# Block-sparse attention on eight cores: the projection of the next head pair moved into the last chunk of the current one, and the block-maximum pass started earlier with doubled buffers

## The chip, the cores and the metric

The kernel runs on the 8 cores of one Trainium2 chip. Every core runs the same program on its own 2 of the 16 sequences, and no core talks to another. The metric is device time in microseconds of the slowest core.

## The reference, cut to what matters

One layer: a layer norm, then attention plus a feed-forward block, both added to the input. The attention is exact on the best-scoring 32x32 blocks and coarse elsewhere.

```
xn = layernorm(x)                       # 16 x 2048 x 1024, 16 heads of 64
Q, K, V = heads(xn @ W.T + b)           # per head: 2048 x 64, 64 blocks of 32 rows
low  = mean(Qb) @ mean(Kb).T * SCALE    # 64 x 64 block scores
hi_mask = the 1024 best blocks (with the diagonal band)
blk_rmax = max of hi scores per row; max_vals = max over the row's chosen blocks
attn = exp(hi - max_vals);  low_attn = exp(low - row_max - 10000*hi_mask) * 32
out  = (hi_out*hi_corr + low_out*low_corr) / (hi_norm*hi_corr + low_norm*low_corr + 1e-6)
x + out + sigmoid(xr @ Wr.T) * (relu(xk @ Wk.T)**2 @ Wv.T)
```

## The kernel before, in words

The program writes the instruction list of each engine by hand, in Python order. `Rec.emit` appends an instruction and, on every engine but TensorE, first makes it wait for the engine's own previous instruction; `Rec.wait` makes an engine wait until another engine's counter has reached a value. There is one counter per engine (sPE, sDV, sAC, sSY for the sync queue's transfers, sGP for GpSimd's transfers, sGC for GpSimd's arithmetic). So each queue runs in program order, and the transfers that GpSimd issues go one at a time: the next is issued when the last has landed.

The first 2255 us (layer norm, weight transposes, block selection by bisection, feed-forward) are not touched by the change. After that a loop over 8 head pairs `p` runs. A pair has four units of attention `bhs[0]` to `bhs[3]` (two heads times two sequences), and goes through these stages:

- **QK projection** (lines 979 to 995): 16 groups of 8 matmuls of 512 columns make `qtp` and `ktp` from the normalised input `xnT`; ScalarE evacuates each group. The groups use the two halves (slots) of the PSUM tile `pA` in turn.
- **V projection and transposes** (from line 1006): twice 4 groups of 8 matmuls of 512 columns into `pA`, evacuated to `vTf` (line 1025), and after each four groups 16 transposing matmuls (line 1045) into `pS` with two ScalarE copies each (lines 1054 and 1058). Between the transposes stands phase A of `bhs[0]`, two units per transpose.
- **Phase A** of one `bhs` (`emit_phaseA_half`, 64 units): a matmul of 512 columns of Q·K into one half of `pA` (line 748), a VectorE maximum over blocks into `bm` (line 756), and after every fourth unit the mask `bx` is added (line 763) and the maximum taken (line 766). After unit 63, VectorE and ScalarE make `eps_all` (lines 771 to 777). `bx` and `rmb` are loaded per `bhs` by `emit_prep_bx` on GpSimd (lines 692 and 696); there is one buffer of each, so the load waits for the end of phase A of the `bhs` before (`phA_done_dv`), and the first unit of a phase A waits for its `bx`.
- **Four chunks** `i` = 0 to 3, one per `bhs`, of 32 iterations `kg` (`emit_chunk_iter`): two score matmuls into `pS` (line 823), the two output matmuls of the iteration before (line 791, `emit_av`, which wait for its exponential), up to two units of phase A of a later `bhs`, and the exponential of 128x1024 on ScalarE (line 838). Halfway and at the end ScalarE evacuates `pO` to `outT` (line 810). `emit_prep` loads the `rhsc` and `lhsc` operands of the next chunk on GpSimd (lines 705 and 707). The epilogue of a chunk transposes and scales; half of it is put off to `kg` 4 of the next chunk. At the end of a pair, GpSimd adds two tiles (lines 950 and 953), the result is stored, and sync, TensorE and VectorE wait for everything.

Units of phase A before, by stage: `bhs[0]` all 64 in the V stage; chunk 0: 64 of `bhs[1]`; chunk 1 from `kg` 8: 48 of `bhs[2]`; chunk 2 from `kg` 8: 16 of `bhs[2]`, then 32 of `bhs[3]`; chunk 3 in `kg` 8 to 23: 32 of `bhs[3]`. In chunk 3 the iterations 24 to 31 have none.

Of the kernel before, what the change touches and what calls it, by code (L numbers as in the profile page):

```python
# [9 lines left out]
F32 = mybir.dt.float32  # L10
# [85 lines left out]
def build_program(debug=False, trunc=None):  # L96
# [36 lines left out]
    with stack:  # L133
# [503 lines left out]
        with contextlib.ExitStack() as st_p2:  # L637
# [15 lines left out]
            bm = sb("bm", [128, 64], F32)  # L653
            bmm = sb("bmm", [128, 64], F32)
            bx = sb("bx", [128, 1024], F32)
            rmb = sb("rmb", [128, 16], F32)
# [15 lines left out]
            def bh_idx(p, hip, s):  # L672
# [9 lines left out]
                     "nac_la": [0, 0], "ngp_prep": [0, 0], "ndv_prep": [0, 0], "ngp_bx": 0,  # L682
                     "nac_la_last": 0, "ngp_prep_last": 0,
                     "prev_exp": [0, 0], "phA_dv": 0, "phA_done_dv": 0,
                     "nst_a": 0, "ngp_rmb": 0, "prev_exp2": [0, 0], "phA_dv2": [0, 0], "nac_ep": 0,
# [3 lines left out]
            def emit_prep_bx(p, hip, sq):  # L689
                b = bh_idx(p, hip, sq)  # L690
                r.wait("gpsimd", "sDV", state["phA_done_dv"])
                state["ngp_bx"] = r.emit("gpsimd", lambda e, b=b: e.dma_start(
                    bx[:, :],
                    bsm_dram[b].rearrange("j t k -> j (t k)")
                    .unsqueeze(1).broadcast_to([4, 32, 1024])))
                state["ngp_rmb"] = r.emit("gpsimd", lambda e, b=b: e.dma_start(
                    rmb[:, :],
                    rm_dram[b].unsqueeze(1).broadcast_to([4, 32, 16])))

            def emit_prep(p, hip, sq, par, prev_chunk_pe, with_bx=False):  # L700
# [7 lines left out]
                    lhs2[par][0:64, :], ktp[p0:p0 + 64, ts0:ts0 + S]))  # L708
                if with_bx:
                    emit_prep_bx(p, hip, sq)  # L710
# [20 lines left out]
                state["ngp_prep"][par] = state["ngp_rmb"]  # L731
                state["ndv_prep"][par] = ngp5

            def emit_phaseA_half(p, hip, sq, u):
                b = bh_idx(p, hip, sq)
                p0 = 64 * hip
# [19 lines left out]
                nred = r.emit("vector", lambda e, kq=kq, half=half: e.tensor_reduce(  # L756
                    bm[:, kq * 16:(kq + 1) * 16],
                    pA[:, half * 512:(half + 1) * 512]
                    .rearrange("p (k e) -> p k e", e=32),
                    axis=AX.X, op=ALU.max))  # L760
                state["phA_dv2"][half] = nred
                if kq == 3:
                    r.emit("vector", lambda e, b=b, t=t: e.tensor_tensor(  # L763
                        bmm[:, :], bm[:, :], bx[:, t * 64:(t + 1) * 64], ALU.add))
# [4 lines left out]
                if u == 63:  # L769
                    r.wait("vector", "sGP", state["ngp_rmb"])  # L770
# [3 lines left out]
                    ndv_e = r.emit("vector", lambda e: e.tensor_tensor(  # L774
                        epst[:, :], epst[:, :], rmb[:, :], ALU.max))
                    r.wait("scalar", "sDV", ndv_e)
                    r.emit("scalar", lambda e, b=b: e.activation(
                        eps_all[:, b * 16:(b + 1) * 16], epst[:, :],
                        AF.Exp, bias=clneps[:, :]))
                    state["phA_done_dv"] = ndv_e  # L780
# [180 lines left out]

            state["nls_next"] = 0
            for p in range(8):
# [7 lines left out]
                r.wait("scalar", "sPE", r.cnt["sPE"])  # L971
                r.wait("scalar", "sGP", r.cnt["sGP"])
                r.wait("tensor", "sSY", nls)
                pcons = state["pcons"]
                for tag, dst in [("q", qtp), ("k", ktp)]:
                    for n in range(8):
                        slot = n % 2
                        r.wait("tensor", "sAC",
                               max(pcons[slot], state["pA_free_ac"][slot]))
                        r.wait("tensor", "sDV",  # L980
# [83 lines left out]
                for i in range(4):  # L1064
# [4 lines left out]
                    for kg in range(32):  # L1069
# [3 lines left out]
                        elif i == 1:  # L1073
                            if kg == 0:
                                emit_prep_bx(*bhs[2])
# [100 lines left out]
```

How the kernel before makes its waits and increments, by code:

```python
    def emit(self, eng, fn):  # L57
        sname = ESEM[eng]
        n = 16 if eng in ("sync", "gpsimd") else 1
        if eng != "tensor" and self.cnt[sname]:
            self.wait(eng, sname, self.cnt[sname])
        self.cnt[sname] += n
        h = self.sem[sname]
        self._push(eng, lambda e, fn=fn, h=h, n=n: fn(e).then_inc(h, n))
        return self.cnt[sname]
# [1 line left out]
    def wait(self, eng, sname, val):  # L67
        if not val:
            return
        h = self.sem[sname]
        self._push(eng, lambda e, h=h, v=val: e.wait_ge(h, v))
```

## Time and profile before

| what | value |
|---|---|
| median of 2 runs | 6025.58 us (6016.91 to 6034.24) |
| the profiled execution | 6024.37 us; span of its slowest core 6022.5 us |
| spans of the 8 cores | 5990.2 to 6022.5 us |
| mean granted TensorE clock, by core | 0.751 to 0.756 of full |
| busy: PE, DVE, ACT | 52%, 41%, 28% of the span |

All views below are of core 1, the slowest. Times are microseconds from the start of its span. PE is TensorE's matmul stream, PEld its weight loads, DVE is VectorE, ACT ScalarE, POOL GpSimd, SPq the sync queue. PEclk is the granted share of TensorE's full clock of 2.4 GHz; 0.50 is 1.2 GHz. An engine that is idle is only a loss where the next thing that ends last stands behind it.

### The profile page before, as it was taken

Reading aid. Unit: us, or ns where it says so; the run is one execution under the profiler, and the core shown is the slowest. Engines: PE = TensorE matmul, PEld = TensorE weight load, DVE = VectorE, ACT = ScalarE, POOL = GpSimd, SP = SyncE. Lnnn points to the kernel's source line nnn. Section 1 sums busy time; section 2 is a strip of 40 time slices with the busy share of each in tenths; the row PEclk is TensorE's granted clock in tenths of the full one; section 3 lists DMA queues with packets and bytes.
Section 4 is the critical chain, followed back from the end, with each engine's and each line's share of the span. In section 5 each row is a group of like instructions: output and inputs, shape, how many; then the busy total and the mean of one; then the engine's idle time right before and its main releaser. Section 6 shows DMA issues by size and latency. Waiting matters only on the chain.

```text
span 6022.5 us, 57635 instructions; the slowest of 8 cores (5990.2 to 6022.5 us)
## 1 busy us (share of the span) xinstructions
PE 3157.4 (52%) x11513; PEld 1112.4 (18%) x11513; DVE 2488.4 (41%) x5263; ACT 1708.7 (28%) x2627; POOL 281.9 (5%) x301
## 2 busy tenths in 40 slices
PE   1121113333333426765766676676676667666676
PEld 0021101111111102221222222122122122122121
DVE  3421224433444224543643543543552642543454
ACT  2200000000000002542442443443344344254254
POOL 0000010000000000000000000000000000000000
PEclk9965556777676856886886887777787787687687
DMA  1233001121111211011010110100110010010010
GB/s 62 67 74 80 2 16 42 42 49 44 40 42 40 61 41 25 20 22 28 17 25 22 24 25 20 25 22 15 25 25 20 18 32 17 21 31 18 17 27 18
DMA packets 516779, 190.09 MB, mean 32 GB/s; under 512 B 494282, under 2 KB 495474, under 8 KB 516274
## 3 DMA queue, kind: packets, MB, share of 16 engines
q1 hardware_dynamic: 482386, 130.46, 9.5%
q0 software_dynamic: 34080, 55.95, 4.2%
q8 instruction: 136, 2.23, 0.2%
q14 instruction: 177, 1.45, 0.1%
HBM read 142.23 MB, written 39.34 MB: 30 GB/s over the span
## 4 chain that ended last, share of the span: by engine, by line
PE 37%; DMA 19%; DVE 17%; ACT 14%; issue 11%; DVEq 1%; POOL 1%; ACTq 1%; SPq 0%; POOLq 0%
PE pA L748 9%; PE pS L823 9%; ACT aT L838 7%; PE pO L791 7%; DVE bm L756 5%; PE pA L984 4%; PE pA L516 4%; DMA bx<-bsm_dram 3%; DMA fW<-wT_r 3%; ACT stage L916 2%; DMA nb<-norm_all 2%; DVE fA L501 2%; DMA fW<-wT_v 2%; DMA fW<-wT_k 2%; PE pA L1017 1%
## 5 line engine op out<-in xcount | busy, mean ns | idle before, releaser
L756 DVE TENSOR_REDUCE bm<-pA 128x16 f32<-128x512 f32 x2048 | 1416.7, 692 | 1321.4 <-PE pA L748 1164.2
L838 ACT ACTIVATE aT<-pS 128x1024 bf16<-128x1024 f32 x1024 | 1048.7, 1024 | 974.1 <-PE pS L823 938.3
L748 PE MATMUL pA<-ktp,qtp 64*128 64x512 bf16 x2048 | 883.3, 441 | 632.2 <-DMA bx<-bsm_dram 252.0
L791 PE MATMUL pO<-aT,vtm 128*65 128x512 bf16 x2048 | 714.7, 435 | 360.5 <-ACT aT L838 358.5
L823 PE MATMUL pS<-rhsc,lhsc 128*128 128x512 bf16 x2048 | 725.4, 443 | 29.0 <-DVE rhsc L712 29.0
L516 PE MATMUL pA<-fA,fW 128*128 128x512 bf16 x1536 | 412.7, 421 | 276.8 <-DMA fW<-wT_r 65.0
L748 PEld LDWEIGHTS pA<-ktp,qtp 64*128 64x128 bf16 x2048 | 190.1, 95 | 1334.3 <-issue 1330.9
L417 PE MATMUL pB<-bis_cnt,ones 128*128 128x32 f32 x116 | 35.1, 397 | 684.3 <-DVE bis_cnt L413 684.3
L791 PEld LDWEIGHTS pO<-aT,vtm 128*65 128x65 bf16 x2048 | 237.9, 124 | 703.8 <-issue 562.3
L516 PEld LDWEIGHTS pA<-fA,fW 128*128 128x128 bf16 x1536 | 151.1, 105 | 533.0 <-issue 421.8
L547 ACT ACTIVATE fR<-pA 128x512 bf16<-128x512 f32 x64 | 38.2, 597 | 675.9 <-PE pA L516 675.9
L984 PE MATMUL pA<-xnT,wsl_q 128*128 128x512 bf16 x512 | 128.6, 418 | 183.3 <-DMA out<-stage 121.1
L823 PEld LDWEIGHTS pS<-rhsc,lhsc 128*128 128x128 bf16 x2048 | 156.7, 107 | 351.6 <-issue 338.6
L1054 ACT ACTIVATE vtm<-pS 128x64 bf16<-128x64 f32 x256 | 57.5, 224 | 417.8 <-PE pS L1045 415.6
L581 ACT ACTIVATE fA<-fB 128x512 bf16<-128x512 bf16 x64 | 40.3, 629 | 475.4 <-DVE fB L574 470.2
L547 ACT ACT_TABLE_LOAD x1 | 1.3, 1283 | 594.7 <-PE pA L516 594.7
L916 ACT ACTIVATE stage<-pA,rdenw 128x64 f32<-128x64 f32 x384 | 120.6, 314 | 134.5 <-DVE rdenw L906 103.1
L417 PEld LDWEIGHTS pB<-bis_cnt,ones 128*128 128x128 f32 x116 | 29.0, 310 | 693.3 <-issue 693.3
L900 DVE TENSOR_TENSOR rdenw<-pA,eps_all 128x8 f32<-128x8 f32 x48 | 8.0, 167 | 319.3 <-PE pA L893 304.2
L763 DVE TENSOR_TENSOR bmm<-bm,bx 128x64 f32<-128x64 f32 x512 | 115.6, 226 | 53.9 <-DVE bm L756 0.9
L766 DVE TENSOR_REDUCE mv_all<-bmm 128x1 f32<-128x64 f32 x512 | 112.6, 220 | 54.8 <-DVE bmm L763 2.8
L1017 PE MATMUL pA<-xnT,wsl_v 128*128 128x512 bf16 x512 | 132.9, 425 | 2.0 <-DVE bm L756 2.0
(145 smaller groups left out, 2326.6 us busy)
## 6 DMA issues: line engine op xcount, KB each, us to landing
xtile<-x SPq DMA_DIRECT2D x64, 512.0 KB
fW<-wT_r SPq DMA_DIRECT2D x64, 256.0 KB
fW<-wT_k SPq DMA_DIRECT2D x64, 256.0 KB
fW<-wT_v SPq DMA_DIRECT2D x64, 256.0 KB
bx<-bsm_dram POOLq DMA_DIRECT2D x32, 512.0 KB, 8.6
out<-stage SPq DMA_DIRECT2D x32, 512.0 KB
rhsc<-qtp POOLq DMA_DIRECT2D x32, 256.0 KB, 2.9
lhsc<-ktp POOLq DMA_DIRECT2D x32, 256.0 KB, 2.9
```

The costliest lines, as they stand in the source:

```text
L501: e.scalar_tensor_tensor(d[:, c * QT:(c + 1) * QT], xnT[:, base:base + QT], mucol[m][:, c:c + 1], d[:, c * QT:(c + 1) * QT], ALU.mult, ALU ...
L516: e.matmul(pA[:, sl * 512:sl * 512 + QT], w[:, cc * 128:(cc + 1) * 128], rb[:, cc * QT:(cc + 1) * QT], start=(cc == 0), stop=(cc == 7)))
L748: e.matmul(pA[:, half * 512:(half + 1) * 512], qtp[p0:p0 + 64, ts0 + t * 128:ts0 + (t + 1) * 128], ktp[p0:p0 + 64, ts0 + kq * 512:ts0 + (k ...
L756: nred = r.emit("vector", lambda e, kq=kq, half=half: e.tensor_reduce(bm[:, kq * 16:(kq + 1) * 16], pA[:, half * 512:(half + 1) * 512] .re ...
L763: r.emit("vector", lambda e, b=b, t=t: e.tensor_tensor(bmm[:, :], bm[:, :], bx[:, t * 64:(t + 1) * 64], ALU.add))
L766: e.tensor_reduce(mv_all[:, b * 16 + t:b * 16 + t + 1], bmm[:, :], axis=AX.X, op=ALU.max))
L791: e.matmul(pO[:, sl * 512:(sl + 1) * 512], vtm[:, (sq * 16 + k) * 130 + hip * 65: (sq * 16 + k) * 130 + hip * 65 + 65], aT[bpar][:, sl * 5 ...
L823: e.matmul(pS[bpar][:, sl * 512:(sl + 1) * 512], lhs2[par][:, k * 128:(k + 1) * 128], rhs2[par][:, qh * 1024 + sl * 512: qh * 1024 + (sl + ...
L838: e.activation(aT[bpar][:, :], pS[bpar][:, :], AF.Exp, scale=0.125))
L916: e.activation(stg[:, i * 64:(i + 1) * 64], pA[:, sl8 * 128:sl8 * 128 + 64], AF.Identity, scale=rdenw16[:, i:i + 1])))
L984: e.matmul(pA[:, slot * 512:(slot + 1) * 512], wsl[tag][:, cc * 128:(cc + 1) * 128], xnT[:, cc * T + n * 512:cc * T + (n + 1) * 512], star ...
L1017: e.matmul(pA[:, slot * 512:(slot + 1) * 512], wsl["v"][:, cc * 128:(cc + 1) * 128], xnT[:, cc * T + n * 512: cc * T + (n + 1) * 512], sta ...
```

## The change

The `bx` mask buffer becomes two of bf16 (it was one of f32), `rmb` and `bm` are doubled too, and the counters that guard them are kept per buffer. The QK projection of a pair is cut into a function for one group. Only pair 0 still runs its 16 groups at the start; those of pair p+1 run in chunk 3 of pair p, one group ahead of each of the iterations `kg` 16 to 31. Phase A starts in the V projection: two units stand after each V group and each transpose, 80 in all: 64 of `bhs[0]`, then 16 of `bhs[1]`. The others move forward: chunk 0 has 48 of `bhs[1]` and 16 of `bhs[2]`, chunk 1 the other 48 of `bhs[2]`, chunk 2 from `kg` 8 48 of `bhs[3]`, chunk 3 in `kg` 8 to 15 the last 16. The masks are loaded a `bhs` earlier. The wait of a chunk for its operands no longer includes the `rmb` transfer.

```diff
-            bx = sb("bx", [128, 1024], F32)
-            rmb = sb("rmb", [128, 16], F32)
+            bx2 = [sb("bx0", [128, 1024], BF), sb("bx1", [128, 1024], BF)]
+            rmb2 = [sb("rmb0", [128, 16], F32), sb("rmb1", [128, 16], F32)]
...
             def emit_prep_bx(p, hip, sq):
                 b = bh_idx(p, hip, sq)
-                r.wait("gpsimd", "sDV", state["phA_done_dv"])
+                bpar = b % 2
+                r.wait("gpsimd", "sDV", state["phA_done_dv"][bpar])
...
-                state["ngp_prep"][par] = state["ngp_rmb"]
+                state["ngp_prep"][par] = ngp_qk
...
                 if u == 0:
-                    r.wait("tensor", "sGP", state["ngp_bx"])
+                    r.wait("tensor", "sGP", state["ngp_bx"][bpar])
...
+            def emit_projqk_group(p, tag, n):
+                pcons = state["pcons"]
+                dst = qtp if tag == "q" else ktp
+                slot = n % 2
+                r.wait("tensor", "sAC",
+                       max(pcons[slot], state["pA_free_ac"][slot]))
+                r.wait("tensor", "sDV",
+                       max(state["phA_dv2"][slot], state["ndv_ep"]))
+                for cc in range(8):
+                    r.emit("tensor", lambda e, tag=tag, n=n, cc=cc, slot=slot:
...
+                npe_p = r.cnt["sPE"]
+                r.wait("scalar", "sPE", npe_p)
+                pcons[slot] = r.emit("scalar", lambda e, tag=tag, n=n, slot=slot,
...
+                if p == 0:
+                    r.wait("scalar", "sPE", r.cnt["sPE"])
+                    r.wait("scalar", "sGP", r.cnt["sGP"])
+                    r.wait("tensor", "sSY", nls)
+                    for tag in ("q", "k"):
+                        for n in range(8):
+                            emit_projqk_group(0, tag, n)
+                    state["nac_qk"] = r.cnt["sAC"]
...
                 emit_prep(*bhs[0], 0, 0, with_bx=True)
+                emit_prep_bx(*bhs[1])
...
+                pre_units = [(bhs[0], u) for u in range(64)] + \
+                            [(bhs[1], u) for u in range(16)]
...
                         vev[n4] = pcons[slot]
+                        pre_phA()
...
                         if i == 0:
-                            units = [(bhs[1], 2 * kg), (bhs[1], 2 * kg + 1)]
+                            if kg == 16:
+                                emit_prep_bx(*bhs[2])
+                            if kg < 24:
+                                u0 = 16 + 2 * kg
+                                units = [(bhs[1], u0), (bhs[1], u0 + 1)]
+                            else:
+                                u0 = 2 * (kg - 24)
+                                units = [(bhs[2], u0), (bhs[2], u0 + 1)]
...
+                            elif kg >= 16 and p < 7:
+                                if kg == 16:
+                                    r.wait("tensor", "sSY", state["nls_next"])
+                                    r.wait("scalar", "sGP", r.cnt["sGP"])
+                                tag = "q" if kg < 24 else "k"
+                                emit_projqk_group(p + 1, tag, kg % 8)
```

On TensorE at the start of pair 1, before. `id_f,outT` are the epilogue's transposes of pair 0, `xnT,wsl` the projections, `id_bf,vTf` the transposes of V, `ktp,qtp` the units of phase A:

```order
L854 MATMUL pS1<-id_f,outT 128x65 x8
L984 MATMUL pA<-xnT,wsl_q 128x512 x64
L984 MATMUL pA<-xnT,wsl_k 128x512 x64
L1017 MATMUL pA<-xnT,wsl_v 128x512 x32
L1045 MATMUL pS0<-id_bf,vTf 128x128
L748 MATMUL pA<-ktp,qtp 128x512 x2
```

At the same place with the change:

```order
L866 MATMUL pS1<-id_f,outT 128x65 x8
L1045 MATMUL pA<-xnT,wsl_v 128x512 x8
L756 MATMUL pA<-ktp,qtp 128x512 x2
L1045 MATMUL pA<-xnT,wsl_v 128x512 x8
L756 MATMUL pA<-ktp,qtp 128x512 x2
L1045 MATMUL pA<-xnT,wsl_v 128x512 x8
L756 MATMUL pA<-ktp,qtp 128x512 x2
L1045 MATMUL pA<-xnT,wsl_v 128x512 x8
L756 MATMUL pA<-ktp,qtp 128x512 x2
L1074 MATMUL pS0<-id_bf,vTf 128x128
```

The 128 matmuls of Q and K are gone from here, and the block of 32 V matmuls is cut into four groups with two units of phase A behind each, in the same two halves of `pA`.

On TensorE in chunk 3 of pair 0 with the change, from the last units of phase A (`kg` 15) on. `rhsc1,lhsc1` are the score matmuls, `aT,vtm` the output matmuls, `laT1,vhp_all` the coarse part that closes half a chunk:

```order
L756 MATMUL pA<-ktp,qtp 128x512 x2
L984 MATMUL pA<-xnT,wsl_q 128x512 x8
L835 MATMUL pS0<-rhsc1,lhsc1 128x512 x2
L803 MATMUL pO<-aT1,vtm 65x512 x2
L812 MATMUL pO<-laT1,vhp_all 65x512 x2
L984 MATMUL pA<-xnT,wsl_q 128x512 x8
L835 MATMUL pS1<-rhsc1,lhsc1 128x512 x2
L803 MATMUL pO<-aT0,vtm 65x512 x2
```

The last three rows repeat to the end of the chunk, 16 groups in all. Before, two units of phase A stand in the place of each group up to `kg` 23, and nothing after that.

On POOL, the transfers of pair 0 before, from the operands of chunk 0 (`rhsc`, `lhsc`) on:

```order
L705 DMA rhsc<-qtp 64x2048
L707 DMA lhsc<-ktp 64x2048
L692 DMA bx<-bsm_dram 128x1x1024
L696 DMA rmb<-rm_dram 128x1x16
L705 DMA rhsc1<-qtp 64x2048
L707 DMA lhsc1<-ktp 64x2048
L692 DMA bx<-bsm_dram 128x1x1024
```

And with the change:

```order
L710 DMA rhsc<-qtp 64x2048
L712 DMA lhsc<-ktp 64x2048
L696 DMA bx0<-bsm_dram 128x1x1024
L701 DMA rmb0<-rm_dram 128x1x16
L696 DMA bx1<-bsm_dram 128x1x1024
L701 DMA rmb1<-rm_dram 128x1x16
L710 DMA rhsc1<-qtp 64x2048
L712 DMA lhsc1<-ktp 64x2048
L696 DMA bx0<-bsm_dram 128x1x1024
```

The mask of `bhs[1]` stands ahead of the operands of chunk 1; the third mask (`bhs[2]`) follows them. The first mask of a pair still stands behind two operand transfers.

## Rows read from the trace of the kernel before

**Rows 1.** The page's head: span of the slowest core, busy time by engine.
```profile
span 6022.5 us, 57635 instructions; the slowest of 8 cores (5990.2 to 6022.5 us)
PE 3157.4 (52%) x11513; PEld 1112.4 (18%) x11513; DVE 2488.4 (41%) x5263; ACT 1708.7 (28%) x2627; POOL 281.9 (5%) x301
```

**Rows 2.** Busy time in stretches of pair 3 (us, (x) instructions; PEclk, DMA share, GB/s).
```profile
core 1: us, PE busy (x) PEld busy (x) DVE busy (x) ACT busy (x) POOL busy (x), PEclk, DMA share, GB/s
3657.10:3686.70 29.60, 29.60 (x128) 13.00 (x129) 1.45 (x4) 10.31 (x15) 0.00 (x0) 0.93 0.00 1
3686.70:3693.60 6.90, 6.90 (x33) 3.14 (x32) 0.00 (x0) 3.10 (x5) 1.08 (x2) 1.00 0.28 58
3693.60:3705.10 11.50, 0.30 (x3) 0.07 (x1) 0.00 (x0) 1.14 (x3) 0.71 (x1) 0.72 0.21 56
3705.10:3737.80 32.70, 21.75 (x47) 4.74 (x48) 24.59 (x46) 6.79 (x30) 0.70 (x1) 0.50 0.01 1
3737.80:3747.30 9.50, 9.48 (x32) 3.75 (x33) 1.11 (x3) 2.06 (x3) 0.00 (x0) 0.72 0.00 0
...
4075.60:4110.60 35.00, 25.87 (x87) 7.80 (x86) 14.45 (x30) 18.71 (x19) 0.00 (x0) 0.90 0.00 1
```

**Rows 3.** Waits in pair 3 (3657 to 4129 us): total, times, longest.
```profile
PE pA L748 <- DMA bx<-bsm_dram: 32.2, 3, 15.5
```

**Rows 4.** Costliest groups: busy, mean ns of one, idle before and its releasers.
```profile
L748 PE MATMUL pA<-ktp,qtp 64*128 64x512 bf16 x2048 | 883.3, 441 | 632.2 <-DMA bx<-bsm_dram 252.0 <-ACT aT L838 119.8 <-ACT vtm L1054 61.7
L763 DVE TENSOR_TENSOR bmm<-bm,bx 128x64 f32<-128x64 f32 x512 | 115.6, 226 | 53.9 <-DVE bm L756 0.9
```

**Rows 5.** Timeline, end of pair 2 and start of pair 3 (start, us, instruction, idle before).
```profile
3650.30 2.12 POOL L953 TENSOR_TENSOR stage<-stage,vTf 128x1024 f32<-128x1024 f32 x1
...
3657.10 6.28 PE L984 MATMUL pA<-xnT,wsl_q 128*128 128x512 bf16 x19 [17.20 <-DMA out<-stage]
...
3660.82 0.69 ACT L991 ACTIVATE qtp<-pA,bcol_q 128x512 bf16<-128x512 f32 x1 [13.27 <-PE pA L984]
```

**Rows 6.** Timeline of POOL, then TensorE, at the first mask of pair 3.
```profile
3688.38 0.55 POOL L705 DMA_DIRECT2D rhsc<-qtp  x1 [35.96 <-ACT laT L728]
...
3705.06 1.03 PE L748 MATMUL pA<-ktp,qtp 64*128 64x512 bf16 x2 [11.20 <-DMA bx<-bsm_dram]
```

**Rows 7.** DMA issues: KB each, median us from issue to landing; above, the transfers near 3700.
```profile
bx<-bsm_dram POOLq DMA_DIRECT2D x1, 512.0 KB, 9.4
...
rhsc<-qtp POOLq DMA_DIRECT2D x32, 256.0 KB, 2.9
```

**Rows 8.** Timeline around the second four V groups of pair 3.
```profile
3736.98 1.49 DVE L756 TENSOR_REDUCE bm<-pA 128x16 f32<-128x512 f32 x2 [0.45 <-PE pA L748]
...
3737.82 9.67 PE L1017 MATMUL pA<-xnT,wsl_v 128*128 128x512 bf16 x32 [0.25 <-DVE bm L756]
...
3747.33 0.22 PE L1045 MATMUL pS<-id_bf,vTf 128*128 128x128 bf16 x1
3747.48 0.39 PE L748 MATMUL pA<-ktp,qtp 64*128 64x512 bf16 x1
...
3747.64 0.69 ACT L1025 ACTIVATE vTf<-pA,bcol_v 128x512 bf16<-128x512 f32 x1 [1.04 <-PE pS L1045]
3748.04 0.69 DVE L756 TENSOR_REDUCE bm<-pA 128x16 f32<-128x512 f32 x1 [8.92 <-PE pA L748]
...
3748.69 0.37 PE L748 MATMUL pA<-ktp,qtp 64*128 64x512 bf16 x1 [0.82 <-ACT vtm L1054]
```

**Rows 9.** Timeline at the first units of chunk 0, pair 3.
```profile
3800.33 1.02 PE L748 MATMUL pA<-ktp,qtp 64*128 64x512 bf16 x2 [15.54 <-DMA bx<-bsm_dram]
3801.08 1.49 DVE L756 TENSOR_REDUCE bm<-pA 128x16 f32<-128x512 f32 x2 [16.62 <-PE pA L748]
```

**Rows 10.** Timeline at the end of phase A of `bhs[3]`, pair 3.
```profile
4093.98 0.60 PE L823 MATMUL pS<-rhsc,lhsc 128*128 128x512 bf16 x2
...
4096.27 0.31 ACT L777 ACTIVATE eps_all<-epst,clneps 128x16 f32<-128x16 f32 x1 [4.46 <-DVE epst L774]
4096.67 2.14 ACT L838 ACTIVATE aT<-pS 128x1024 bf16<-128x1024 f32 x2
...
4097.84 0.78 PE L791 MATMUL pO<-aT,vtm 128*65 128x512 bf16 x2 [3.26 <-ACT aT L838]
```

**Rows 11.** Busy time in three stretches of pair 3, columns as in Rows 2.
```profile
3657.10:3660.50 3.40, 3.40 (x9) 1.20 (x10) 1.45 (x4) 0.00 (x0) 0.00 (x0) 0.50 0.00 0
3673.10:3686.70 13.60, 13.60 (x64) 6.16 (x63) 0.00 (x0) 5.50 (x8) 0.00 (x0) 1.00 0.00 1
...
4101.50:4108.50 7.00, 5.66 (x23) 1.76 (x22) 0.00 (x0) 5.98 (x6) 0.00 (x0) 1.00 0.00 0
```

More of the change, by code:

```diff
@@ L755, in emit_phaseA_half @@
                 r.wait("vector", "sPE", npe_a)
[L756 to L760, printed above, removed]
+                nred = r.emit("vector", lambda e, kq=kq, half=half, bmp=bmp:
+                              e.tensor_reduce(
+                                  bmp[:, kq * 16:(kq + 1) * 16],
+                                  pA[:, half * 512:(half + 1) * 512]
+                                  .rearrange("p (k e) -> p k e", e=32),
+                                  axis=AX.X, op=ALU.max))
                 state["phA_dv2"][half] = nred
                 if kq == 3:
[L763 to L764 removed]
+                    r.emit("vector", lambda e, t=t, bmp=bmp, bpar=bpar:
+                           e.tensor_tensor(bmm[:, :], bmp[:, :],
+                                           bx2[bpar][:, t * 64:(t + 1) * 64],
+                                           ALU.add))
                     r.emit("vector", lambda e, b=b, t=t:
@@ L997, in build_program, with pre_phA @@
                 r.wait("gpsimd", "sAC", r.cnt["sAC"])
                 emit_prep(*bhs[0], 0, 0, with_bx=True)
+                emit_prep_bx(*bhs[1])
                 vsl = [(pS[0], 0), (pS[0], 512), (pS[1], 0), (pS[1], 512)]
                 vcons = [0] * 4
-                u_phA = 0
+                pre_units = [(bhs[0], u) for u in range(64)] + \
+                            [(bhs[1], u) for u in range(16)]
+                upos = [0]
+                def pre_phA():
+                    for _ in range(2):
+                        if upos[0] < 80:
+                            emit_phaseA_half(*pre_units[upos[0]][0],
+                                             pre_units[upos[0]][1])
+                            upos[0] += 1
@@ L1073, in build_program @@
                         elif i == 1:
                             if kg == 0:
-                                emit_prep_bx(*bhs[2])
+                                emit_prep_bx(*bhs[3])
+                            if kg >= 8:
+                                u0 = 16 + 2 * (kg - 8)
+                                units = [(bhs[2], u0), (bhs[2], u0 + 1)]
+                        elif i == 2:
                             if kg >= 8:
                                 u0 = 2 * (kg - 8)
-                                units = [(bhs[2], u0), (bhs[2], u0 + 1)]
-                        elif i == 2:
-                            if kg == 16:
-                                emit_prep_bx(*bhs[3])
+                                units = [(bhs[3], u0), (bhs[3], u0 + 1)]
+                        else:
```

86 lines of the change are left out of this document (35 added, 51 removed).

## The prediction, made before the changed kernel had run

> **What bounds the kernel now.** I read the page's head first: no engine is busy much over half of the span, TensorE 52%, VectorE 41% [rows 1], so the time lies in hand-overs and waits, and has to be read stage by stage. I then cut pair 3 into stretches with the busy-time view [rows 2]. Its stages differ in what ends last. The 128 projection matmuls of Q and K fill TensorE: 29.6 us busy in 29.6 us. The 11.5 us after the first V groups hold almost nothing (PE 0.30). In the transposes with phase A, VectorE is busy 24.59 of 32.7 us. At the end of chunk 3, TensorE (25.87 of 35.0) and ScalarE (18.71) both have room, but TensorE's share holds units of phase A that have to run somewhere. The view of waits says what stands behind the empty stretches: in pair 3 the phase-A matmuls wait three times for the `bx` transfer, 32.2 us in all [rows 3]. Over the run it is 252.0 us [rows 4], or 31.5 per pair, so pair 3 is typical and I work from it.
>
> **The change part by part, for a middle pair (1 to 6).**
>
> *Q and K leave the start:* −29.6 us [rows 2].
>
> *The start of the pair.* V begins where Q began (3657.10, Rows 5), at 1.2 GHz: a group of 8 matmuls takes 3.4 us there [rows 11] against 6.9/4 = 1.73 at 2.4 GHz [rows 2]. The first unit now waits for the first mask, whose transfer still stands behind two operand transfers. That chain took 3705.06 − 3688.38 = 16.7 us [rows 6]. With nothing left to wait for on ScalarE, it can start when POOL's last add ends, at 3650.30 + 2.12 = 3652.4 [rows 5], so the first unit runs at 3669.1, 12.0 us after V began. Behind it is a handshake that was not there: V groups and units share the two halves of `pA`. An even group needs the half that the unit just before it filled, and the next unit needs the half of that group. Its links:
>
> - group start to ScalarE's evacuation: 3660.82 − 3657.10 = 3.72 us at 1.2 GHz [rows 5]. At 2.4 GHz the evacuation starts 0.31 after the next matmul (3747.33 to 3747.64), so 2.04;
> - evacuation 0.69, then 3748.69 − 3748.33 = 0.36 until the unit starts [rows 8];
> - unit to maximum 0.75 at 1.2 GHz [rows 9], 0.56 at 2.4 (3747.48 to 3748.04); two maxima 1.49; end of a maximum to the next V group 0.15 (3737.67 to 3737.82) [rows 8].
>
> Where a group waits for both maxima: 3.72 + 0.69 + 0.36 + 0.75 + 1.49 + 0.15 = 7.2 us at 1.2 GHz, 5.3 at 2.4. Where it only follows the second unit: 3.72 + 0.69 + 0.36 + 0.43 = 5.2, or 3.3. They alternate, 12.4 us per two groups, or 8.6. Which clock is granted there the trace cannot show. The nearest rows are the transposes with phase A, 0.50, and the four V groups behind them, 0.72 [rows 2]. I take 0.72, linearly between: 10.7. From the first unit to the second V group it is 0.75 + 1.49 + 0.15 = 2.4, then three groups, 15.1 (17.6 at 1.2 GHz, 11.9 at 2.4). The transposes so start 12.0 + 2.4 + 15.1 = 29.5 us after V, where it was 6.9 + 11.5 = 18.4: **+11.1** (+13.6 or +7.9).
>
> *The second four V groups:* 2 × 10.7 = 21.4 instead of 9.5, **+11.9** (+15.3 or +7.7). The transposes themselves carry as many units as before and cost the same.
>
> A page of the Trainium skill, "TensorE: Matmul & The Clock Gate", section "A second HAM failure mode: psum-queue depth-cycling", says that small idles between matmul groups make the clock swing between its two levels. Rows 2 agree for like work (0.50 and 0.72), and by that rule neither of the two bounds would hold throughout.
>
> *The other two mask waits.* The masks of `bhs[1]` and `bhs[3]` are loaded a `bhs` ahead, so 32.2 − 11.2 = **−21.0** [rows 3, 6]. What is late next there is VectorE, which then runs its maxima without a gap. The pause at the end of a phase A, where ScalarE's exponential queues behind `eps_all`, leaves ScalarE idle for 4.46 us [rows 10]; there are four per pair in both kernels, only at other places (from chunk 2 into chunk 1, the others within their stage).
>
> *Chunk 3, `kg` 16 to 31.* Each iteration gets a group of 1.73 us. With two score and two output matmuls that is 12 × 0.2157 = 2.59 us at 2.4 GHz, with ScalarE at 2.14/2 + 0.69 = 1.76 [rows 10, 8], so TensorE bounds. Dense matmuls held 1.00: 64 in 13.6 us [rows 11]. From the point of the row at 4093.98 [rows 10] the pause holds the first output matmuls until 4097.84, 3.9 us, of which the first group hides 1.7. The closing matmuls, the evacuation of `outT` and the next exponential, with the second group beside them, end some 4 us later: 7.9 for two iterations. Fourteen more take 36.3, the tail (exponential, four matmuls, evacuation) 3.5: 47.7 us instead of 35.0 [rows 2], **+12.6** (+9.9 if TensorE never waits, 16 × 2.59 + 3.5; +17 if the first two iterations run at 1.2 GHz). The ScalarE order puts the group's evacuation ahead of the exponential; the next output matmuls stand a full group later, which hides it.
>
> *Unknown costs.* The bf16 mask is not in the trace. Its transfer lands after between 2.9 us (`rhsc`, 256 KB) and 9.4 (`bx` now) [rows 7]. I keep 9.4, as rows, sources and their count are unchanged; 2.9 would take 6.5 from the first wait, 52 us over 8 pairs. The add of a bf16 mask costs 226 ns now [rows 4]; I cost the new type at nothing, within 20 ns either way, 10 us over 512 of them.
>
> *Sum.* Middle pair: −29.6 + 11.1 + 11.9 − 21.0 + 12.6 = −15.0, six of them −90. Pair 0 keeps its Q and K, and its first mask waits for them as before; its first unit comes when it did, and the handshake is added: 2.4 + 15.1 + 11.9 − 21.0 + 12.6 = +21. Pair 7 has no next projection: chunk 3 loses eight iterations' units, and iterations without units run at 7.0/6 = 1.17 us [rows 11]; I get 27.9 for the 35.0, −7.1. So 11.1 + 11.9 − 29.6 − 21.0 − 7.1 = −35. Together −104, from the profiled execution's 6024.4: 5920.7, say **5921 us**. That execution is 1.2 us from the median of the runs, so no correction is made.
>
> **Rivals.**
>
> 1. *The handshake runs at 1.2 GHz throughout.* A middle pair is then −29.6 + 13.6 + 15.3 − 21.0 + 12.6 = −9.1, pair 0 +27, pair 7 −29, together −57: 5968 us. For it: 0.50 in the transposes [rows 2]. Against: the V groups are long dense runs, and 0.72 behind the same transposes. By the page's rule above it would not stay there.
>
> 2. *2.4 GHz throughout, or a faster mask.* All at 2.4: −22.4, +14, −42, together −163: 5861 us; the mask at 2.9 us would make it 5810 at the lowest. For it: chunk work with gaps gets 0.90 [rows 2]. Against, for the mask: it took 9.4 us for 512 KB where the operands took 2.9 for 256, so bytes are not what sets it. "DMA: Bandwidth & Descriptors", in "Why a DMA increments its semaphore by 16 and not by 1", a page of the Trainium skill, says that the outer dimensions set how many DMA engines share a transfer. They are unchanged here, and by that rule the transfer is not halved.
>
> 3. *The masks' waits stay:* a load a `bhs` ahead is queued behind something and the 21.0 us remain. Then −104 + 168 = +64: 6088 us. Against: POOL is idle from the first masks until chunk 0, and each mask now needs a buffer freed a `bhs` before.
>
> 4. *Slower: chunk 3 becomes TensorE's bound at a low clock.* If dense matmuls beside ScalarE's load are granted 1.2 GHz in `kg` 16 to 31, an iteration takes 5.18 instead of 2.59, 41 us more in each of seven pairs, +290: about 6210 us. It decides from 2.59 + 104/7/16 = 3.5 us per iteration on, a mean granted clock of some 0.74. For it: the Q and K stretch had 0.93, not 1.00 [rows 2]. Against: that is the cold start, and the rest of the stretch has 1.00 [rows 11].
>
> **How the numbers follow.** Chances: the forecast 0.50, rival 1 0.20, rival 2 0.22, rival 3 0.03, rival 4 0.05. Two per cent, about what a measurement of this kernel can tell from no change, is 120 us: faster means below 5905. The forecast lies 16 us above that, and a mean clock of 0.8 or a few us less per pair cross it, so about a third of its chance falls there; with nearly all of rival 2 that is 0.38. Slower is rival 4, 0.05. The rest is 0.57. For the range I go from between the forecast and rival 2's far end to beyond rival 1: 5845 to 5985, with rivals 3, 4 and the lowest corner outside.
>
> **What would show it.** In the changed profile: TensorE waiting for `bx` some 8 us per pair, once, and nowhere else; the stretch from the first V group to the first transpose near 29.5 us and the second four groups near 21, at a clock between 0.5 and 1; chunk 3's second half near 48 us, with TensorE nearly full at 1.00; pair 0 longer than before, pair 7 shorter by some 35 us. It is wrong if mask waits remain in chunks 0 or 2, if the V groups take less than 15 us per four, or if an iteration with a group takes over 3 us.

## The result, and the profile after

The changed kernel takes 5982.75 us (median of 9 runs, 5977.38 to 5993.23) against 6018.78 for the kernel before: a ratio of 0.9937, 95% interval 0.9926 to 0.9948. It is faster, by 36 us or 0.6%, where 5921 us was forecast, 1.7% below. The profiled execution took 5972.39 us, a little less than the nine runs; that is 52.0 us less than the profiled one before, half of the forecast's 104. The account by stages below explains these 52 us, not the 36 of the medians.

The head of the changed kernel's page, which answers to [rows 1]; below it the groups and the mask's transfer that answer to [rows 4, 7]:

```profile
span 5970.8 us, 57629 instructions; the slowest of 8 cores (5939.9 to 5970.8 us)
...
PE 3215.4 (54%) x11513; PEld 1121.1 (19%) x11513; DVE 2489.0 (42%) x5263; ACT 1708.7 (29%) x2627; POOL 280.1 (5%) x301
...
L756 PE MATMUL pA<-ktp,qtp 64*128 64x512 bf16 x2048 | 892.0, 447 | 488.4 <-ACT aT L850 110.6
...
L1045 PE MATMUL pA<-xnT,wsl_v 128*128 128x512 bf16 x512 | 212.9, 591 | 175.6 <-DMA out<-stage 130.6
...
bx<-bsm_dram POOLq DMA_DIRECT2D x32, 256.0 KB, 7.4
```

The `bx` transfer is gone as the first releaser of the units, whose idle time fell from 632.2 to 488.4 us. In pair 3 the view of waits has one wait for it left, as forecast, where [rows 3] has three:

```profile
PE pA L756 <- DMA bx<-bsm_dram: 6.9, 1, 6.9
```

But PE is busier by 58 us with the same 11513 matmuls, so part of them ran at a lower clock. Busy time in stretches of pair 3 of the changed kernel (core 5; columns as in [rows 2]): first V matmul to first transpose, the transposes, the second four V groups, chunk 0 in halves, and the projection in chunk 3:

```profile
core 5: us, PE busy (x) PEld busy (x) DVE busy (x) ACT busy (x) POOL busy (x), PEclk, DMA share, GB/s
3679.60:3709.40 29.80, 17.21 (x40) 4.84 (x40) 6.66 (x13) 3.10 (x5) 2.78 (x4) 0.65 0.15 21
3709.40:3743.30 33.90, 21.85 (x49) 4.87 (x48) 25.70 (x48) 7.23 (x32) 0.00 (x0) 0.52 0.00 1
3743.30:3767.30 24.00, 17.20 (x40) 4.87 (x40) 6.43 (x12) 2.75 (x4) 0.00 (x0) 0.61 0.00 1
3801.70:3841.60 39.90, 32.66 (x105) 9.12 (x104) 29.53 (x57) 17.67 (x18) 2.00 (x4) 0.85 0.16 27
3841.60:3882.80 41.20, 31.90 (x100) 9.25 (x101) 25.37 (x49) 17.79 (x19) 0.55 (x1) 0.82 0.02 4
...
4090.00:4120.00 30.00, 30.00 (x140) 13.93 (x139) 0.00 (x0) 20.11 (x24) 0.00 (x0) 1.00 0.00 1
```

The last row is the projection beside chunk 3: PE full, at 1.00. The first and the third row are the price of the units between the V groups: 29.8 us from the first V matmul to the first transpose, and four V groups that took 9.5 us at 0.72 [rows 2] take 24.0 at 0.61. The timeline of that stretch shows the turns on `pA` (answers to [rows 8]):

```profile
3743.37 3.57 PE L1045 MATMUL pA<-xnT,wsl_v 128*128 128x512 bf16 x8 [0.22 <-DVE bm L765]
...
3747.10 0.69 ACT L1053 ACTIVATE vTf<-pA,bcol_v 128x512 bf16<-128x512 f32 x1 [5.27 <-PE pA L1045]
3748.14 1.02 PE L756 MATMUL pA<-ktp,qtp 64*128 64x512 bf16 x2 [1.20 <-ACT vTf L1053]
3748.90 1.49 DVE L765 TENSOR_REDUCE bm<-pA 128x16 f32<-128x512 f32 x2 [4.22 <-PE pA L756]
3750.53 3.57 PE L1045 MATMUL pA<-xnT,wsl_v 128*128 128x512 bf16 x8 [1.36 <-DVE bm L765]
...
3755.81 3.33 PE L1045 MATMUL pA<-xnT,wsl_v 128*128 128x512 bf16 x8
...
3762.51 3.38 PE L1045 MATMUL pA<-xnT,wsl_v 128*128 128x512 bf16 x8 [1.19 <-DVE bm L765]
```

PE waits 1.20 us for ScalarE, then 1.36 for VectorE, and starts again. The groups start 7.16, 5.28 and 6.70 us apart. The prediction's links gave 7.2 and 5.2 at 1.2 GHz, 5.3 and 3.3 at 2.4: the first two turns are the low-clock sums, the third lies between.

The table below is used in all that follows. It holds the stages in us, means over pairs 1 to 6 on the slowest core, from the start times in the traces (V: first V matmul; T: first transpose; V2: the second four V groups). Its last row is the median of the runs.

| stage | before | change | masks_only | qk_back | noshake | v_in_ps | mask_early | ps_early | v_fill |
|---|---|---|---|---|---|---|---|---|---|
| V to T | 7.2 | 27.9 | 6.9 | 35.5 | 8.7 | 20.4 | 23.0 | 12.0 | 26.9 |
| T to V2 | 43.2 | 34.0 | 42.6 | 34.0 | 33.5 | 34.1 | 34.0 | 34.3 | 33.3 |
| V2 | 9.3 | 23.7 | 8.9 | 23.4 | 9.2 | 11.9 | 23.8 | 11.1 | 20.3 |
| second T | 36.6 | 34.2 | 36.6 | 34.2 | 36.7 | 34.8 | 34.2 | 34.9 | 33.7 |
| chunk 0 | 91.0 | 80.6 | 75.9 | 81.0 | 76.2 | 79.3 | 81.0 | 80.9 | 79.9 |
| chunk 1 | 75.9 | 80.8 | 75.9 | 81.3 | 77.9 | 80.7 | 81.3 | 80.8 | 80.8 |
| chunk 2 | 86.8 | 75.5 | 80.5 | 75.1 | 85.3 | 75.3 | 75.5 | 75.4 | 75.0 |
| chunk 3, epilogue | 82.1 | 94.8 | 82.4 | 76.5 | 101.3 | 96.1 | 95.0 | 94.9 | 95.1 |
| to next V (with Q, K where they stand there) | 39.9 | 11.0 | 38.7 | 38.9 | 11.0 | 10.8 | 10.9 | 10.7 | 11.0 |
| pair | 472.1 | 462.6 | 448.4 | 480.0 | 439.7 | 443.7 | 458.6 | 434.9 | 456.0 |
| median | 6019 | 5983 | 5858 | 6103 | 5802 | 5828 | 5949 | 5771 | 5943 |

### The profile page after: what moved, and what is told of

The parts are those of the page before. It is cut to its first block, busy times and chain, and to the rows that moved or that the text cites. A ratio compares the mean times of both kernels' runs of the same rounds, so it can differ in the third digit from the quotient of the medians.

```text
span 5970.8 us, 57629 instructions; the slowest of 8 cores (5939.9 to 5970.8 us)
## 1 busy us (share of the span) xinstructions
PE 3215.4 (54%) x11513; PEld 1121.1 (19%) x11513; DVE 2489.0 (42%) x5263; ACT 1708.7 (29%) x2627; POOL 280.1 (5%) x301
## 4 chain that ended last, share of the span: by engine, by line
PE 38%; DVE 18%; DMA 16%; ACT 14%; issue 11%; DVEq 1%; ACTq 1%; POOL 0%; SPq 0%; POOLq 0%
PE pA L756 9%; PE pS L835 8%; PE pO L803 7%; ACT aT L850 7%; DVE bm L765 5%; PE pA L984 3%; PE pA L1045 3%; PE pA L516 3%; DMA fW<-wT_r 3%; ACT stage L928 2%; DMA fW<-wT_k 2%; DMA fW<-wT_v 2%; DMA nb<-norm_all 2%; DVE fA L501 2%; DVE bis_ge L409 1%
## 5 line engine op out<-in xcount | busy, mean ns | idle before, releaser
L756 PE MATMUL pA<-ktp,qtp 64*128 64x512 bf16 x2048 | 892.0, 447 | 488.4 <-ACT aT L850 110.6
L1045 PE MATMUL pA<-xnT,wsl_v 128*128 128x512 bf16 x512 | 212.9, 591 | 175.6 <-DMA out<-stage 130.6
L1053 ACT ACTIVATE vTf<-pA,bcol_v 128x512 bf16<-128x512 f32 x64 | 44.0, 687 | 363.1 <-PE pA L1045 363.0
```

The lines of the kernel that those rows point to most:

```text
L756: e.matmul(pA[:, half * 512:(half + 1) * 512], qtp[p0:p0 + 64, ts0 + t * 128:ts0 + (t + 1) * 128], ktp[p0:p0 + 64, ts0 + kq * 512:ts0 + (k ...
L1045: e.matmul(pA[:, slot * 512:(slot + 1) * 512], wsl["v"][:, cc * 128:(cc + 1) * 128], xnT[:, cc * T + n * 512: cc * T + (n + 1) * 512], sta ...
```

## The experiments

### The parts of the change one at a time

**masks_only** is the kernel before with the doubled bf16 masks and their earlier loads (and the chunks' wait without the `rmb` transfer):

```diff
-            bx = sb("bx", [128, 1024], F32)
+            bx2 = [sb("bx0", [128, 1024], BF), sb("bx1", [128, 1024], BF)]
...
                 emit_prep(*bhs[0], 0, 0, with_bx=True)
+                emit_prep_bx(*bhs[1])
```

> The kernel before with one edit of the change alone: masks in bf16, doubled buffer, loads issued a chunk ahead; projections and units stand where they stood before. Theory (the masks' waits were real, and the change gives their gain back at the V groups): some 17 us less per pair than before, about 5885 us, below the whole change. Rival (behind each mask wait stands another wait that ends almost as late): within 40 us of the kernel before, above 5980 us.

Measured: 5857.99 us, ratio 0.972 (0.970 to 0.974). This one edit of three gains 162 us, over four times the 36 of the whole change. From the second transposes to the end of chunk 2 it takes 21.4 us off a pair (290.3 to 268.9); the prediction's −21.0 for the waits is right. The rival falls.

**qk_back** is the changed kernel with Q and K at the start of each pair again:

```diff
-                if p == 0:
...
+                        emit_projqk_group(p, tag, n)
...
-                            elif kg >= 16 and p < 7:
+                            elif kg >= 99:
```

> The changed kernel with the projection of Q and K put back to the start of every pair, and the second half of chunk 3 without it. Theory (the move takes 29.6 us off the start and puts 12.8 us on chunk 3): 16.8 us more for each of seven pairs, about 6100 us, and the stretch between the last evacuation of a pair and its first projection back near 9.5 us. Rival (the move is worth nothing, since chunk 3 gives all of it back): about 5980 us.

Measured: 6102.63 us, ratio 1.013 (1.010 to 1.015), slower than the kernel before. A pair has 17.4 us more than with the change. So the move of Q and K gains what the prediction gave it. Beside masks_only, this kernel differs only in where the units run: +245 us, 31 per pair. That third edit, the new places of the units, eats most of what the other two gain.

**noshake** takes the units out from between the V groups, and runs those that this leaves over in chunks 1 to 3:

```diff
                         vev[n4] = pcons[slot]
-                        pre_phA()
...
+                            if kg >= 5:
+                                g0 = (i - 1) * 54 + 2 * (kg - 5)
+                                units = [(bhs[2 + g // 64], g % 64)
+                                         for g in (g0, g0 + 1) if g < 128]
```

> The changed kernel without the mask units between the V groups: the eight V groups of a pair stand alone again, the transposes carry the 64 units of the first chunk, and the 128 units that are left over run two per iteration from iteration 5 on in chunks 1 to 3. Theory (the units and the V groups take turns on the two halves of one PSUM tile, and that costs some 12 us at the start of a pair and 14 us at the second four groups): the second four groups fall from 23.7 to about 9.5 us, first V group to first transpose from 27.9 to about 8 us, some 5 us come back in iterations 5 to 7 of the later chunks; about 28 us less per pair, in all about 5760 us. Rival (the cost of that stretch is the low granted clock, which the kernel has there with or without units): the V groups stay above 15 us per four and the time above 5950 us.

Measured: 5801.54 us, ratio 0.963 (0.961 to 0.966). V2 is back at 9.2 and V to T at 8.7, so the theory holds; but against the change, chunks 2 and 3 are 9.8 and 6.5 us longer (chunks 0 and 1 4.4 and 2.9 shorter), not 5 in all. In chunk 2 the end of a phase A now holds up the exponentials: the one of `kg` 9 starts 6.46 us after the one of `kg` 8 (means of pairs 1 to 6). That is five iterations behind the pause of 6.62 us that stands there anyway, and the iterations behind both are slow (up to 3.17 us).

**v_in_ps** leaves the order as in the change and gives V another PSUM tile:

```diff
-                                   e.matmul(pA[:, slot * 512:(slot + 1) * 512],
+                                   e.matmul(vps[:, voff:voff + 512],
                                             wsl["v"][:, cc * 128:(cc + 1) * 128],
```

> The changed kernel with the V groups' results put into the four 512-column slots of the score tile, which is idle there, in place of the two halves that the units use; order of the units unchanged. Theory (it is the turn-taking on the two shared halves): the second four groups come down from 23.7 to between 9 and 17 us, the start of a pair from 27.9 to about 20 us, some 20 us less per pair, about 5820 us. Rival (the units' own work or the low clock sets the pace, whatever tile V goes to): second four groups at 20 us or above, about 5980 us.

Measured: 5827.63 us, ratio 0.969 (0.964 to 0.974). The busy view of V to T and V2 in pair 3 of v_in_ps (columns as above):

```profile
core 1: us, PE busy (x) PEld busy (x) DVE busy (x) ACT busy (x) POOL busy (x), PEclk, DMA share, GB/s
3620.40:3640.70 20.30, 13.54 (x40) 4.17 (x40) 6.18 (x12) 2.69 (x5) 2.09 (x3) 0.64 0.21 30
3674.80:3686.50 11.70, 11.70 (x41) 3.78 (x40) 5.90 (x12) 2.37 (x4) 0.00 (x0) 0.80 0.00 0
```

The same eight units beside the same 32 V matmuls take 11.7 us with PE full, where they took 24.0. It is the sharing of the two halves that costs, not the units' work.

### The first mask, and where the spare units could go

**mask_early** loads the first mask in chunk 2 of the pair before; **ps_early** is that edit on top of v_in_ps:

```diff
-                emit_prep(*bhs[0], 0, 0, with_bx=True)
+                if p == 0:
+                    emit_prep_bx(*bhs[0])
+                emit_prep(*bhs[0], 0, 0)
...
+                        if i == 2 and kg == 8 and p < 7:
+                            emit_prep_bx(p + 1, 0, 0)
```

> The changed kernel with the first mask of a pair loaded during chunk 2 of the pair before, in place of at the pair's start. Theory (the first unit still waits for its mask: first V group to first unit 9.7 us, where eight matmuls of the V group take about 5): some 5 us less at the start of each pair but the first, about 35 us less than the changed kernel, 5948 us. Rival (the V groups' turns set that stretch, so that units which can start earlier only wait later): first V group to first transpose stays near 27.9 us, about 5983 us.

> The V groups in the score tile and the first mask loaded a chunk ahead of its pair. Theory: the two gains add, 5828 us less 35 us, about 5793 us. Rival (with V in tiles of its own the units wait for nothing but the V groups' own matmuls): within 10 us of 5828 us.

Measured: 5949.23 us, ratio 0.987 (0.984 to 0.991), and 5770.95, ratio 0.958 (0.954 to 0.963). Behind the turns the mask is worth the 5 us expected (27.9 to 23.0): the first unit starts 5.0 us after V in place of 9.7. With V in a tile of its own it is worth 8 (20.4 to 12.0), and the first unit starts after 3.5 us in place of 10.4. Both theories hold; in ps_early the gains add to more than was expected.

**third** takes noshake's free V groups and puts the 16 spare units into chunk 2, a third one per iteration; **third_early** adds the early mask:

```diff
                             elif kg >= 16:
-                                u0 = 2 * (kg - 16)
-                                units = [(bhs[3], u0), (bhs[3], u0 + 1)]
+                                u0 = 3 * (kg - 16)
+                                units = [(bhs[3], u0 + j) for j in range(3)]
```

> Masks and the moved projection of Q and K as in the change, no units between the V groups; all units stand as in the kernel before, except that chunk 2 takes three units in place of two in each iteration of its second half, so that chunk 3 is clear of them when Q and K begin. Theory (the parts add up: masks alone 5858 us, moving Q and K 17 us per pair for seven pairs): 5739 us, and 16 more units in chunk 2 at some 0.4 us each (an iteration with two units takes 1.97 us, one without 1.17) put 6.4 us on each of eight pairs, so about 5790 us, below the 5802 us of the kernel that starts its units earlier. Rival (three units do not fit under one iteration, since they share two PSUM halves): over 16 us more per pair, 5870 us or above.

> The kernel with three units per iteration in chunk 2, and with the first mask of a pair loaded at the start of chunk 3 of the pair before. Theory: the transposes' first unit no longer waits for its mask; the transposes that follow the V groups gain some 5 us per pair, 35 us less than the same kernel without it, about 5755 us. Rival (the V groups alone take as long as the mask's load): no more than 10 us less.

Measured: 5963.67 us, ratio 0.990 (0.987 to 0.992), and 5958.67, 0.989 (0.985 to 0.993). The theory falls, the rival holds in both. An iteration with three units takes 4.27 us, one with two 1.70 and 2.24 in turn. The busy view of that stretch in pair 3 of third:

```profile
3975.00:4025.00 50.00, 39.10 (x83) 8.52 (x82) 28.75 (x54) 11.59 (x12) 0.00 (x0) 0.50 0.00 1
```

And one iteration in its timeline:

```profile
3991.15 1.03 PE L756 MATMUL pA<-ktp,qtp 64*128 64x512 bf16 x2
3991.93 1.49 DVE L765 TENSOR_REDUCE bm<-pA 128x16 f32<-128x512 f32 x2 [0.98 <-PE pA L756]
...
3993.08 0.58 PE L756 MATMUL pA<-ktp,qtp 64*128 64x512 bf16 x1 [0.90 <-DVE bm L765]
...
3993.60 1.03 PE L835 MATMUL pS<-rhsc,lhsc 128*128 128x512 bf16 x2
...
3994.43 1.06 PE L803 MATMUL pO<-aT,vtm 128*65 128x512 bf16 x2
```

The third unit waits 0.90 us for the half that the first one's maximum still reads, and PE stays at 1.2 GHz throughout. With the V groups off the units' path, the early mask is worth nothing: from the first V matmul to V2 it is 42.4 us with it and 42.3 without.

### Wait or clock?

**third_between** moves the first of the three units between score and output matmuls; **between_c1** has the three units in chunk 1 instead:

```diff
                 npe_s = r.cnt["sPE"]
+                if len(units) == 3:
+                    emit_phaseA_half(*units[0][0], units[0][1])
+                    units = units[1:]
```

> The kernel with three units per iteration in the second half of chunk 2, where the first of the three now stands between the score matmuls and those of the output, so that the third finds its PSUM half free. Theory (the 4.27 us of an iteration there come from the third unit's wait for the half that the first one's reduction still reads, 0.90 us per iteration, and from the granted clock of 0.50 that goes with it): the wait goes, the clock of that stretch returns to about 1.00, an iteration takes about 2.6 us (three reductions and their share of the sums on DVE), the half chunk 69.2 less 27 us, about 5750 us in all. Rival (three units are too much work for one iteration, in whatever order): 4 us or more per iteration, about 5960 us. Between them (the wait goes, the clock stays at 0.50): about 3.4 us, 5850 us.

> The same order of three units, in the second half of chunk 1 in place of chunk 2; chunk 1 then ends with the last unit of its sequence, chunk 2 holds two units per iteration as in the changed kernel. Theory (the pause behind a sequence's last unit costs the same wherever it falls, and an iteration with three units too): the same time as with the three units in chunk 2, within 25 us. Rival (a pause that ends with the chunk is hidden behind the pause that every chunk has at its start): 4 us less per pair, 32 us in all.

Measured: 5874.54 us, ratio 0.975 (0.973 to 0.978), and 5871.39, 0.974 (0.972 to 0.977). This is the case between: the wait went, an iteration takes 3.46 us, and the clock did not move. In chunk 1 the three units cost the same, as the theory of between_c1 has it. The stretch in pair 3 of third_between:

```profile
3960.00:3995.00 35.00, 33.28 (x74) 6.77 (x74) 22.32 (x42) 10.00 (x10) 0.00 (x0) 0.50 0.00 1
```

PE is busy 33.28 of 35.00 us and gets half of its clock, while chunk 3's projection gets all of it when full. A unit's matmul has operands of 64 rows (`64*128` in the views), the projection's have 128. **rep_score** and its control **rep_unit** each add two matmuls to these iterations, of 128 and of 64 rows; they write again what is there:

```diff
-                for sl in range(2):
+                for sl in [0, 1] * (2 if len(units) == 3 else 1):
```

> The kernel with three units per iteration and the first of them between the matmuls, with the two score matmuls of those iterations issued twice (the second pair writes the same values again). Each iteration there has 9 matmuls in place of 7; the two more use all 128 rows of the array, a unit's uses 64. Theory (the granted clock stays at 0.50 in that stretch, with PE 95% busy, because three of the seven matmuls use half of the array's rows): the clock comes up to about 1.00, an iteration falls from 3.46 to about 2.6 us, faster with more work, about 5770 us. Rival (the clock does not care): 9 matmuls at 0.43 to 0.49 us, 3.9 to 4.4 us per iteration, about 5950 us.

> The control to the kernel with the doubled score matmuls: the matmuls of the first two units of each three-unit iteration are issued twice, so 9 matmuls too, the two more with 64 rows. Theory (rows): the clock stays at 0.50, 3.9 to 4.4 us per iteration, about 5950 us. Rival (the number of matmuls, or how closely they follow each other, brings the clock up): about 2.6 us, 5770 us.

Measured: 5812.67 us, ratio 0.965 (0.959 to 0.970), and 5947.58, 0.987 (0.981 to 0.993). The stretch in rep_score:

```profile
3928.00:3964.00 36.00, 28.32 (x105) 8.57 (x105) 26.55 (x51) 11.66 (x12) 0.00 (x0) 0.98 0.01 1
```

and in rep_unit:

```profile
3975.00:4025.00 50.00, 48.09 (x110) 8.50 (x110) 29.08 (x55) 12.29 (x12) 0.00 (x0) 0.58 0.00 1
```

The first iterations of that stretch still ran at full clock. On core 1, where the clock had fallen before, a part of the same stretch reads:

```profile
3975.00:4000.00 25.00, 24.71 (x52) 4.03 (x51) 13.89 (x26) 5.13 (x6) 0.00 (x0) 0.50 0.01 1
```

Nine matmuls per iteration in both. With the 128-row ones the clock is 0.98, an iteration takes 3.15 us instead of 3.46, and the kernel is 62 us faster with more work than third_between. With the 64-row ones it falls to 0.50 though PE is busy 24.71 of 25 us, and the kernel is 73 us slower. Theory and control agree on the clock; the size was off (2.6 us expected), as at full speed the units wait for VectorE and the halves again (PE is busy 28.32 of 36.00 us).

**v_fill** asks the same of the changed kernel's V groups:

```diff
                         vev[n4] = pcons[slot]
-                        pre_phA()
+                        for fill in range(6):
+                            if fill == 3:
+                                pre_phA()
+                            r.emit("tensor", lambda e, n=n, vps=vps, voff=voff:
+                                   e.matmul(vps[:, voff:voff + 512],
```

> The changed kernel with six more matmuls of 128 rows behind each V group (three ahead of the two units, three behind them), into slots of the score tile that nothing reads: they fall into the two waits of each turn, 1.20 us for ScalarE and 1.36 us for VectorE. Theory (the turns are slow because the granted clock is low, and the clock is low because PE waits): the clock of the V groups comes up from 0.61 to near 1.00, the second four groups fall from 23.7 us towards the 17.2 us that the prediction worked out for full speed, about 10 us less per pair over both halves, 5900 us. Rival (the clock stays, and the added matmuls stand in line): 6 x 4 x 0.43 us = 10.3 us of matmuls against some 10 us of waits in the second four groups, so 24 to 34 us there, 5985 to 6100 us.

Measured: 5942.71 us, ratio 0.987 (0.984 to 0.990), 40 us less than the change although 384 matmuls were added. V2 in pair 3 of v_fill:

```profile
3731.50:3752.00 20.50, 18.17 (x64) 6.17 (x65) 6.61 (x13) 2.75 (x4) 0.00 (x0) 0.86 0.00 0
```

The clock comes from 0.61 to 0.86 and V2 from 23.7 to 20.3 us, about half of the way to 17.2. The rival falls, and the theory gets 40 of its 83 us. So of the 14.4 us that V2 lost, at least 3.4 are the clock; v_in_ps gets 11.8 of them back by taking the turns away.

**ps_early_some** doubles the score matmuls of ps_early in 15 iterations per pair behind a pause:

```diff
+                for sl in [0, 1] * (2 if len(units) == 2 and kg % 16 in (1, 2, 3) or par == 0 and hip == 0 and kg in (23, 24, 25)
```

> The kernel with the V groups in the score tile and the early mask, with the score matmuls issued twice in the 15 iterations per pair that follow a pause with units in them (1 to 3 and 17 to 19 of chunk 0, 23 to 25 of chunk 0, 17 to 19 of chunks 1 and 2). Theory (full-height matmuls bring the clock back sooner): the iterations at 2.7 to 3.3 us behind each pause shrink to two of that kind in place of three, 1 us less per pause, about 5 us per pair, 5730 us. Rival (the pause itself sets when the clock returns, the doubled matmuls only add 0.43 to 0.87 us each): 6 to 13 us more per pair, 5820 to 5870 us.

Measured: 5759.48 us, ratio 0.956 (0.954 to 0.958), the lowest median, but not apart from ps_early: a pair has 434.6 us against 434.9. The second iteration behind the middle of chunk 0 shrinks (2.74 to 2.09 us), while the first at the chunk's start grows (3.28 to 4.13). The traces show that the theory is right on the clock: in the three iterations behind the middle of chunk 0 it was 0.80, 0.53 and 0.83 and is 1.00 in all three (means of pairs 1 to 6). But the 15 iterations together take 37.0 us of a pair where they took 37.1. What the clock gives, the doubled matmuls take.

## Why the prediction was half right

The terms of a middle pair, as forecast and in the table. **Q and K:** −29.6 against −28.9. **Start of the pair to V2:** +11.1 against +11.5. That it fits is luck, as its errors cancel: the first unit starts 9.7 us after V, not 12.0, in part because the mask's transfer took 7.4 us (I kept 9.4). Against that, the turns behind it take 18.2 instead of 17.5, the transposes from the first unit on take 34.0 where they took 33.0, and the stretch before was 17.4 in the mean, not the 18.4 of pair 3. **Mask waits:** −21.0 against −19.2. **Chunk 3 with its epilogue:** +12.6 against +12.7; qk_back confirms the pair of Q and K terms by itself. **Second V groups:** +11.9 against +14.4. The sum is −9.5, not −15.0. Over all eight pairs, V2 makes up some 22 of the 52 us that are missing and the mask waits 19.

The step that failed is the clock of the handshake: "Which clock is granted there the trace cannot show … I take 0.72, linearly between". The links were right to 0.1 us in the first two turns, but the stretch got 0.61. By the same line 0.61 gives 23.1 us instead of 21.4, and 23.7 were measured. The rows that I interpolated from were not of like work: 0.72 belonged to 32 dense 128-row matmuls [rows 2], and the new stretch has waits between its groups and 64-row units in them. Pair 4 alone of the middle pairs was granted 0.78, and there the same four groups took 21.4 us (20.5 by that line):

```profile
4206.80:4228.20 21.40, 14.35 (x40) 4.48 (x41) 6.42 (x12) 2.75 (x4) 0.00 (x0) 0.78 0.00 1
```

v_fill shows that this clock can be moved, and by what. Rival 1, the handshake at 1.2 GHz throughout, put V2 at 24.8 us and the whole at 5968, nearer than the forecast. By the rule of the Trainium skill that the prediction cited, "TensorE: Matmul & The Clock Gate", section "A second HAM failure mode: psum-queue depth-cycling", neither level would hold throughout; the trace agrees, with 0.61.

The mask waits are the second miss, 1.8 us per pair. masks_only has −21.4 in the same stages, so the waits went, and it is the units' new order that gives some back. Where, the means of pairs 1 to 6 tell. The second transposes are 2.4 us shorter than in masks_only, but the first exponential of chunk 0 starts 4.5 us behind the first score matmul, not 1.4, which takes that back and 0.7 more. The 21 iterations behind it lose another 1.5 us. At the start of chunk 0 in pair 3, an instruction that ScalarE has ahead of the exponential waits for VectorE; first the change, then masks_only:

```profile
3805.71 0.35 ACT L734 ACTIVATE laT<-la_t,cln 64x64 bf16<-64x64 f32 x1 [5.23 <-DVE la_t L731]
3745.53 0.35 ACT L734 ACTIVATE laT<-la_t,cln 64x64 bf16<-64x64 f32 x1 [1.73 <-DVE la_t L731]
```

I called the pauses at a phase A's end equal wherever they fall, and that held in the sum: the one that moved out of chunk 2 costs chunk 1 5.0 us and saves chunk 2 5.0. That of chunk 0 moved from its last iterations to `kg` 23, and the iterations behind it take 3.08 and 2.47 us where 1.70 and 2.24 are usual; that is 0.8 us more in all, and the end of the chunk gives 0.7 back. The busy view of the changed kernel behind that pause in pair 3:

```profile
3863.00:3871.00 8.00, 7.62 (x21) 1.87 (x19) 4.64 (x9) 3.48 (x4) 0.00 (x0) 0.69 0.00 0
3871.00:3882.00 11.00, 8.24 (x30) 2.50 (x30) 8.21 (x16) 5.16 (x6) 0.55 (x1) 0.98 0.00 0
```

PE is nearly full at 0.69 in the first row; in the second the clock is back, and it has room.

The ends of the loop make up the rest. Cut at the first V matmul, the prediction's +21 and −35 for pairs 0 and 7 read −8.6 and −5.4, since the 29.6 us of Q and K fall to the pair before; measured are −2.8 and +7.7. In pair 7 the mask term gave −14.4 of its −21.0, chunk 3 −5.3 of −7.1, and V2 cost 15.4. Six pairs at 5.5 us, and 5.8 and 13.1 for the ends, are the 52 us that are missing.

Rivals 3 and 4 are refuted: one wait for `bx` per pair is left, and an iteration with a group takes 2.59 us at 1.00. Of rival 2's two halves, the faster mask came true in small: the median is 7.4 us for half the bytes, 8.6 us at 512 KB before. That the transfer would not be halved held. But the Trainium skill's "DMA: Bandwidth & Descriptors", section "Why a DMA increments its semaphore by 16 and not by 1", says only how many engines share a transfer; that its time therefore stays was my own step, and what sets these 7.4 us no run here shows.

## What to carry to other kernels

When work is put into the gaps of another stream, look first at which buffers the two would take in turns: the new places of the units cost 31 us per pair, and 19 of them came back when V alone got a PSUM tile apart, in the same order (155 us in all). Run the parts of a large change one at a time; here one of three, alone, gained 2.8% where the whole gained 0.6%. And price TensorE work at the clock of the mix that it will stand in, not at the clock of the same instructions elsewhere.

## What was not expected of the hardware

TensorE's granted clock does not follow PE's busy time alone. With three of seven matmuls on 64 rows it stayed at 0.50 over 35 us in which PE was busy 95%; with two more 128-row matmuls per iteration it was 0.98, with two more 64-row ones it fell to 0.50. The profile counts a matmul to its modelled end; by their starts, 0.43 us apart, the nine of rep_unit still fill 3.8 of the 4.1 us of an iteration. The Trainium skill's "TensorE: Matmul & The Clock Gate", section "What's actually happening", says that the clock is set by how busy the PE has been recently. Read as the busy time of the profile, these runs do not agree with it. What it is in the two kinds of matmul that counts (rows, or something that goes with them) was tried in this one pair only. Chunk iterations with two units come back to 0.98 (the rows behind the pause, above), so a third unit makes the difference between a stretch that recovers and one that does not; where the limit lies stays open.
